# First adapter added to each tile of x instead of being folded into the weight product, and the sums of weight blocks made in one group instead of two

## The reference

```python
# layer 0: adapter alone, chosen for each batch by an id
x = x + ((x @ B0[id0].T) @ A0[id0].T)
# layer 1: weight, bias and adapter
x = x + (x @ W.T + b) + ((x @ lora_A[id1]) @ lora_B[id1]) * 2.0
```

## Time and profile before

| | |
|---|---|
| three runs | 1396.95, 1397.52, 1401.27 us |
| median | 1397.52 us |
| profiled execution | 1398.88 us, span 1396.9 us |
| mean granted TensorE clock | 0.997 |
| TensorE busy | 1372.8 us, 98% of the span |
| VectorE, ScalarE busy | 943.6 us (68%), 529.1 us (38%) |
| moved by DMA | 311.60 MB, mean 223 GB/s |

### The profile page before, as it was taken

One profiled execution on the slowest core, in us unless ns is written; L12 is line 12 of the kernel. 1 busy time (PEld: TensorE's weight loads), 2 busy tenths in 40 slices (PEclk: granted clock), 3 DMA queues, 4 the chain that ended last, 5 costly groups with the idle time before them and its releaser, 6 DMA issues.

```text
span 1396.9 us, 16200 instructions
## 1 busy us (share of the span) xinstructions
PE 1372.8 (98%) x6024; PEld 1128.8 (81%) x6024; DVE 943.6 (68%) x1049; ACT 529.1 (38%) x588; POOL 79.1 (6%) x163
## 2 busy tenths in 40 slices
PE   6899999999999999999999999999999999999999
PEld 5788877888888878888888888888888888888887
DVE  4677897777877887687765566665755566665662
ACT  3444444433334443343324453333233444333321
POOL 2012010001010000001001000000101000000000
PEclk9999999999999999999999999999999999999999
DMA  9789764778888987599895335455856343555642
GB/s 343 242 293 306 264 238 147 243 236 282 297 292 307 314 297 264 178 301 327 287 358 194 110 112 180 163 175 168 276 204 189 117 135 134 169 167 189 194 151 83
DMA packets 98591, 311.60 MB, mean 223 GB/s; under 512 B 13009, under 2 KB 14289, under 8 KB 98513
## 3 DMA queue, kind: packets, MB, share of 16 engines
q1 hardware_dynamic: 92736, 298.96, 63.1%
q0 software_dynamic: 5776, 11.61, 2.9%
HBM read 254.94 MB, written 55.57 MB: 222 GB/s over the span
## 4 chain that ended last, share of the span: by engine, by line
PE 91%; DVE 4%; DMA 2%; issue 1%; ACT 1%; SPq 1%; ACTq 0%; DVEq 0%
PE acc L590 27%; PE acc L591 27%; PE acc L592 27%; DMA w_two<-w 2%; PE acc L565 2%; PE down_ps L549 2%; PE down_ps L550 2%; PE image_ps L535 1%; PE image_ps L529 1%; PE image_ps L530 1%; DVE w_one L759 1%; DVE bg_lo L794 1%; DVE w_lo L767 1%; DVE x_lo L789 0%; ACT w_hi L627 0%
## 5 line engine op out<-in xcount | busy, mean ns | idle before, releaser
L590 PE MATMUL acc<-x_hi,w_hi 128*128 128x512 f32 x1792 | 702.1, 392 | 16.3 <-DVE x_lo L789 12.5
L591 PE MATMUL acc<-x_lo,w_hi 128*128 128x512 f32 x1792 | 699.5, 390 | 0.0
L592 PE MATMUL acc<-x_hi,w_lo 128*128 128x512 f32 x1792 | 699.1, 390 | 0.0
L627 ACT ACTIVATE w_hi<-w_one 128x1024 fp32r<-128x1024 f32 x223 | 235.9, 1058 | 541.1 <-PE acc L592 504.5
L767 DVE TENSOR_TENSOR w_lo<-w_one,w_hi 128x1024 fp32r<-128x1024 f32 x223 | 273.1, 1225 | 215.2 <-ACT w_hi L627 215.2
L590 PEld LDWEIGHTS acc<-x_hi,w_hi 128*128 128x128 f32 x1792 | 337.6, 188 | 89.0 <-issue 16.6
L591 PEld LDWEIGHTS acc<-x_lo,w_hi 128*128 128x128 f32 x1792 | 337.6, 188 | 71.7 <-issue 1.0
L592 PEld LDWEIGHTS acc<-x_hi,w_lo 128*128 128x128 f32 x1792 | 337.3, 188 | 71.2
L660 ACT ACTIVATE sums<-acc 128x512 f32<-128x512 f32 x96 | 57.1, 594 | 203.7 <-PE acc L592 188.1
L826 DVE SCALAR_TENSOR_TENSOR sums<-acc,bias_sb,sums 128x512 f32<-128x512 f32 x128 | 95.7, 747 | 22.0 <-PE acc L565 20.8
L759 DVE TENSOR_TENSOR w_one<-w_one,w_two 128x1024 f32<-128x1024 f32 x79 | 96.4, 1220 | 17.1 <-DMA w_two<-w 17.1
(11 more groups left out here) (61 smaller groups left out, 610.3 us busy)
## 6 DMA issues: line engine op xcount, KB each, us to landing
w_one<-w SPq DMA_DIRECT2D x143, 512.0 KB, 5.5
w_one<-w_sums SPq DMA_DIRECT2D x80, 512.0 KB, 3.7
w_two<-w SPq DMA_DIRECT2D x79, 512.0 KB, 7.4
x_stage<-x SPq DMA_DIRECT2D x64, 512.0 KB, 4.4
out<-sums SPq DMA_DIRECT2D x128, 256.0 KB, 4.6
w_sums<-w_one SPq DMA_DIRECT2D x40, 512.0 KB, 4.1
resident<-x SPq DMA_DIRECT2D x32, 512.0 KB, 8.6
bg_raw<-w_rows SPq DMA_DIRECT2D x32, 512.0 KB, 5.0
```

What stands on the lines that cost most here:

```text
L590: pe.matmul(ps[:, :], w_hi[ws][:, c, :], hi, start=(c == 0), stop=False)
L591: pe.matmul(ps[:, :], w_hi[ws][:, c, :], lo, start=False, stop=False)
L592: mm = pe.matmul(ps[:, :], w_lo[ws][:, c, :], hi, start=False, stop=(c == H - 1))
L627: act.activation(w_hi[s % W_PARTS][:, :, :], w_one[s % W_ONES][:, :, :], ACT.Copy).then_inc(w_hi_ready, 1)
```

## The change

Two things change, and the order tables with them.

1. The sums of W blocks are made in group 0 only and stored there (`KEPT_IN` is 0 for all); groups 1 to 3 load them.
2. The images of A0 through W are gone, with their 32 loads of `w_rows`, the splits and their matmuls. Instead, for each batch, an "up" projection (`project_up`: one matmul of 512 columns for each of the 16 tiles of 128 columns, L653) computes the first adapter's share, and VectorE (`add_up`) adds it from PSUM to the piece of x. Half of the pieces lie in `resident`; for each group 8 others (2 batches, 4 each) pass through `bg_raw`, are stored to a new DRAM tensor `x1` and loaded again where products 2, 3, 5 and 6 need them. Only the cross term of the two adapters is left of the images: 4 matmuls with `across` (`make_image`), steps 6 to 9.

So a batch's down projection, which needs all 16 tiles of x, must be complete before its x can be used: that of batch 1 stands ahead of step 0, and those of a later group move into products 4 to 6 of the group before.

```diff
-KEPT_IN = {0: 1, 1: 1, 2: 1, 4: 1, 6: 1}
+KEPT_IN = {0: 0, 1: 0, 2: 0, 4: 0, 6: 0}
...
+def downs(s):
+    if s >= STEPS:
+        return []
+    if s < 3:
+        first = (0, 8, 10, 13, 16)
+        return list(range(first[s + 1], first[s + 2]))
...
+def ups(s):
...
+    if s < 0:
+        return [0, 1]
+    g, i, o = where(s)
+    found = [2, 3] if s == 0 else []
+    if i == 0:
+        found += [16 * g + 4 * A0 + r for r, at in enumerate((1, 2, 4, 5) if g else (4, 4, 5, 5)) if at == o]
+    found += [16 * g + 4 * B0 + r for r, at in enumerate((7, 8, 10, 11)) if at == s % PER_GROUP]
...
+            def store_x1(v):
+                y = RAW["up", v]
+                n, half, r = up_chunk(v)
+                sp.wait_ge(up_added, 2 * v + 2)
+                sp.dma_start(x1[n][:, 2 * r:2 * r + 2, :], bg_raw[y % 2][:, :, :]).then_inc(x1_stored[y % 2], DMA)
...
+            def project_up(v):
...
+                for u in range(2):
+                    e = 2 * v + u
+                    if e >= 2:
+                        pe.wait_ge(up_added, e - 1)
+                    o = 2 * r + u
+                    pe.matmul(up_ps[e % 2][:, :], up_w[:, P * o:P * (o + 1)], rank_x_of(n)[:, :], start=True, stop=True)\
+                      .then_inc(up_done, 1)
...
+            def split_chunk(d):
+                wait_for_down_source(act, d)
+                for e in (2 * d, 2 * d + 1):
+                    if e >= 11:
+                        act.wait_ge(bg_used, e - 2)
+                    act.activation(down_parts(e)[0], down_source(e), ACT.Copy).then_inc(bg_hi_ready, 1)
...
+            for d in (5, 6, 7):
+                split_chunk(d)
+            make_w(1)
+            add_down(1)
+            split_rank_x(1)
+            for v in range(CH):
+                add_up(v)
+                split_x(0, v)
+            split_down(0)
+            for d in downs(0):
+                split_chunk(d)
```

More of the change, by code:

```diff
@@ L73, in turn @@
     return 2 * (n // 2) + 1 - n % 2
-def background(s):
+DOWN_STAGED = (2, 3, 14, 15)
+B1, A0, B0, A1 = range(4)
+def downs(s):
     if s >= STEPS:
         return []
+    if s < 3:
+        first = (0, 8, 10, 13, 16)
+        return list(range(first[s + 1], first[s + 2]))
     g, i, o = where(s)
[L81 to L90, removed]
@@ L93, in chunk @@
[L93 to L111, removed]
-def raw_loads(y):
-    return sum(raw_slot(u) == raw_slot(y) for u in range(y + 1))
@@ L119, in raw_before @@
[L119 to L126, removed]
-RANK_SPLIT = {(2, 7): 3, (4, 0): 4, (5, 0): 5, (6, 0): 6}
+    if g + 1 < GROUPS and H * 4 <= s % PER_GROUP < H * 5:
+        return [16 * (g + 1) + o]
+    if g + 1 < GROUPS and H * 5 < s % PER_GROUP <= H * 6:
+        return [16 * (g + 1) + 8 + s % PER_GROUP - H * 5 - 1]
@@ new lines, in down_chunk, with up_chunk, up_resident, down_resident @@
+def down_chunk(d):
+    return turn(d // 8), d % 8
+def up_chunk(v):
+    g, rest = divmod(v, 16)
+    part, r = divmod(rest, 4)
+    return 2 * g + (part in (B1, B0)), int(part in (B1, A1)), r
+def up_resident(v):
+    return v % 16 // 4 in (B1, A0)
+def down_resident(d):
+    n, k = down_chunk(d)
+    return n < 2 and (k >= 4) == (n == 1)
+RAW = {}
+for _s in range(-1, STEPS):
+    for _d in downs(_s):
+        if not down_resident(_d) and _d not in DOWN_STAGED:
+            RAW["down", _d] = len(RAW)
+    for _v in ups(_s):
+        if not up_resident(_v):
+            RAW["up", _v] = len(RAW)
@@ L130, in has_sum @@
+UP_SPLIT = {2: 1}
+UP_LOAD = {}
+for _g in range(GROUPS):
+    _s = PER_GROUP * _g
+    if _g:
+        UP_LOAD[_s - 15], UP_SPLIT[_s - 12] = 4 * _g + B1, 4 * _g + B1
+        UP_LOAD[_s - 7], UP_SPLIT[_s - 1] = 4 * _g + A0, 4 * _g + A0
+    UP_LOAD[_s + (3 if _g == 0 else 0)], UP_SPLIT[_s + 6] = 4 * _g + B0, 4 * _g + B0
+    UP_LOAD[_s + 7], UP_SPLIT[_s + 12] = 4 * _g + A1, 4 * _g + A1
+DOWN_AFTER = ((1, 3, 5), (5, 6))
+IMAGE_STEP = 6
 def has_sum(s):
@@ L443, in _ @@
                     store(s - 2)
[L444 to L449 removed]
+                for v in ups(s + 1):
+                    if not up_resident(v):
+                        load_raw("up", v)
+                if s + 2 >= CH:
+                    for d in downs(s + 2):
+                        load_raw("down", d)
             for s in (STEPS - 2, STEPS - 1):
@@ L499, in _ @@
                     .then_inc(a0_loaded, DMA)
-            for j in range(4):
-                load_rows(j)
-                if j:
-                    keep_image(j - 1)
+            load_up(1)
+            for n in range(NB):
+                pool.dma_start(rows[R * n:R * (n + 1), :], adapter(1, n, b1).rearrange("u r d -> (u r) d"))\
+                    .then_inc(b1_rows_loaded, DMA)
             for s in range(STEPS):
                 g, i, o = where(s)
-                if s + 4 in FIRST:
+                if s + 4 in FIRST and s:
@@ L775, in sum_x @@
                 if i == 1:
-                    for k in range(2):
-                        dve.wait_ge(resident_loaded[k][r], DMA * (g + 1))
+                    dve.wait_ge(up_added, up_number(p, r))
+                    if g == 0:
+                        dve.wait_ge(bg_ready, 32)
                     if last_staged(p, r) >= 0:
```

520 lines of the change are left out of this document (289 added, 231 removed).

## The result

The changed kernel took 1413.27 us (median of 4 runs, 1413.06 to 1415.06), the kernel before 1397.38 in the same comparison: ratio 1.011, interval [1.0091, 1.013]. It is slower by 1.1%, 14 us more than the 1399 forecast and 1 us above the upper end of the range.

A forecast was written before the change was run, and what follows sets the result against it. TensorE, busy 98% of the span, was taken as the bound. Step 1 at 55.5, matmuls of 1330.2 and 3.7 at the end made 1389.4; waits of 2, 3 and 4.2 gave 1398.6, median 1399 us, range 1387 to 1412.

The forecast's parts named there:

- The matmul count and its price: Whole kernel: 5816 matmuls from step 1 on at 0.2275 us each, 1323.1 us; 17.6 us less from matmuls removed and added.
- The start: Ahead of step 1: batch 1's down and up projections come first, so step 1 starts at 55.5, 34.7 us later.
- Waits in group 0: Group 0 after the start: three new waits of TensorE, 2, 3 and 4.2 us, 9.2 together.
- Steps 4 and 5: Group 0: the second up piece waits for VectorE's add of the first, behind `w_lo` and the sum; 3 us, ends 0 and 6.
- R1: Rival, slower: transfers set group 0's pace at 331 GB/s, wait 11 us, clock falls twice; 1412 us, chance 0.33.
- Transfers: Loops 9 to 20 of group 0: loads and stores run 11.2 us behind, 4.2 us of it waits; ends 0 and 11.
- the 7 us of cover: Group 0: transfer delay taken as hidden by weights issued early, VectorE's spare time and landing times; 7 us.
- Steps 1 and 2: Group 0: three down pieces a step with three half buffers make ScalarE's splits wait; 2 us for both, ends 0 and 5.
- R3: Rival, slower: VectorE bounds the first steps, in-order waits in product 0 cost 7 us more; 1406 us, chance 0.07.

The follow-up runs named there:

- e3: The kernel before with the sums of products 1, 2, 4 and 6 stored in group 0 and not made again in group 1: 1404.27 us.
- e4: The changed kernel with VectorE adding the two up shares ahead of the weights' sum in loops 4 and 5: 1409.85 us.
- e5: The changed kernel with the split of `up_w` put first in loop 6 and the four image-row copies at the start of their loops: 1414.74 us.
- e7: The changed kernel with a second new order ahead of step 0, all four up pairs before step 0 and the second weights' sum later: 1407.51 us.
- e10: The changed kernel with the orders of e7 and e4, two banks for image matmuls, the second sum and lora_A copy moved: 1402.57 us.
- e12: e11 with the copy of lora_A back at its old place on ScalarE, ahead of batch 0's rank rows: 1392.19 us.
- e6: The changed kernel with each sum's store cut to an eighth; groups 1 to 3 load one W block instead of the stored sum: 1407.25 us.
- e2: The changed kernel with sums of W blocks made in groups 0 and 1 and stored in group 1 only: 1415.05 us.
- e9: The changed kernel with the sums of products 1 and 2 made in every group and never stored: 1408.27 us.
- e1: The changed kernel with a first new order ahead of step 0, all down pieces split before the first weights are summed: 1410.19 us.
- e11: e10 and e9 together, so the sums of products 1 and 2 are not stored: 1395.33 us.

## Why the prediction was wrong

**What held.** The matmul count and its price: groups 1 to 3 took 989.9 us against 989. The start: 56.7 against 55.5, with the chain in the order given, 39.7 for the first step against 38. The adds are hidden in groups 1 to 3, and nothing came back in group 1 for the sums it no longer makes (e3 tested that part alone).

**The step that failed** is "Waits in group 0", three terms that came to 9.2 us. Group 0 lost 19.2 there:
- "Steps 4 and 5": the mechanism was right (e4 removed most of it), the size was not. 3 us were put, 6.9 measured. The add was late as worked out (1.9 us waited at 85.98), but batch 0's rank rows were late too, 1.4 us, and after these two waits the matmuls ran at the half clock, about 1.5 us (5.7 lost in step 4, against 4.2 in e5 and e7 with the same waits and no fall). The term left the clock out, although R1 priced it.
- Steps 7 and 8 had no term at all; they lost 4.6. Two new things meet there: the up matmul waits for `up_w`, whose last part stands behind the weights' sum on VectorE, and the second and third image matmuls wait for the copy of the one before out of the same bank. I had called the image matmuls unchanged. They stay four, but move from between the image pieces of four different steps to one bank in four steps in a row. Two banks took 3 us of the 4.6 away (e10, e12), the order of the copies 0.3 (e5).
- "Transfers": 4.2 put, 6.2 measured in steps 15 to 24, by the mechanism given. e6 shows that it is the bytes of the sums' stores, e2 that it moves with them, e9 that it goes with 16 of them. I had the rate as 350 GB/s; the stretches showed 370 and 344. So the rate was nearly right. That the 7 us of cover were too generous by 2 is the likely reading, and no run measured the cover.
- "Steps 1 and 2": 2 put, 0.6 measured.

The rest of the miss is 1.2 us of start, 1.3 spread over the rest of the span, and 1.6 between span and median: the median came 2.2 above the profiled span, where 0.6 had been put.

One of the prediction's own signs came: it called itself wrong if waits in steps 6 to 55 passed 8 us. The waits listed there are 8.4 us, the losses 11.7.

**The rivals.** The time came out where R1 had it, 1412, but for R1 in its own words (transfers set the pace) it is only a third right: 6.2 of the 19.2 us are transfers, and the clock fell in step 4, behind waits for VectorE. That the number agrees is luck. 11.5 us are lost in steps 4 to 8 by in-order waits for VectorE and by a bank, which is nearest to R3, priced 7 us and given a chance of 0.07; R3 named neither step 8 nor the bank. Taken together the forecast summed three waits at middling values, each with its upper end at 5, 6 and 11. The one of steps 4 and 5 came out above its upper end (6.9), the transfers in the middle (6.2), steps 1 and 2 near nothing, and one that was not on the list added 4.6. A dense stretch with four new kinds of work, all in order on three engines, should have weighed more than 0.40 together on the slow side.

**The Trainium skill** on transfers ("DMA: Bandwidth & Descriptors", "Bandwidth") gave 1394 by its 425 GB/s and 1397 by its 358. The changed kernel, with loads and stores, ran at 370 with the engines full and at 344 over the next 60 us, on both sides of the lower figure, so in such a mix the lower figure is the closer one; by neither figure would the steps 4 to 8 have been seen.

**What stays open.** Step 4 still loses 2.8 us and step 7 1.6 in the best version. Why two waits of the same lengths brought the half clock in the changed kernel and not in e5 and e7 isn't shown. The start is still 27 us behind the kernel before, and no run here tried to shorten its chain of single instructions (fewer copies for `rank_x`, a smaller first piece), so how much of that is bound to the scheme isn't known. Nor was the second order tried with fewer up pairs ahead of step 0.

## What to carry to other kernels

Replacing a large piece of work by a smaller one in a kernel that is bound by one engine brings only the difference on that engine (here 17.6 us), while each new dependence costs where the engine idles at the start or where an in-order queue puts a producer behind other work; list every new instruction that the bound engine waits for, with what stands ahead of it on its own engine, also those whose number does not change. Work saved on an engine that isn't the bound was worth nothing by itself here (e3), but it can be spent: making 48 sums again in place of storing and loading them took the bytes out of the stretch that was short of them. When a wait is removed by moving an instruction, look at what now stands behind it; four such moves here (in e1, e5, e7 and e10) gave some or all of their gain back close by.

## What the runs showed of the hardware

A mix of loads and stores of 512 KB ran at 370 GB/s with all DMA engines busy (120 to 160 in the changed kernel), and at 392 in a stretch in which they were mostly loads (the first row below). Whether TensorE waited did not follow from the rate alone: it waited for no transfer at 298 to 301 (e6), nor in the 40 us at 370, was idle 3.9 of the next 60 us at 344 (the changed kernel), and not at all in 25 us at 359 in the kernel before.

After waits of 1.4 and 1.9 us within 4 us, with six product matmuls between them, the granted clock was 0.83 over the ten microseconds from 80 to 90 in the changed kernel. In e7 TensorE had the same two waits with the same six matmuls between them, and the granted clock was 1.00 (second row). In e11 one wait of 2.36 us was followed by a granted clock of 0.51 over 7 us (third row), with matmuls 0.43 us apart. So waits shorter than the one of 2.84 us can bring the half clock, and the same waits don't always.

ScalarE's copy of 16 partitions by 1024 took 1.05 us, as long as one of 128 partitions (1.06), so the three pieces of `up_w` cost three full copies.

```profile
20.00:30.00 10.00, 6.14 (x13) 3.96 (x14) 8.78 (x12) 4.72 (x7) 2.16 (x4) 0.58 1.03 392
...
70.00:90.00 20.00, 16.60 (x87) 13.48 (x86) 13.86 (x17) 7.37 (x9) 1.46 (x3) 1.00 0.75 238
...
77.00:84.00 7.00, 6.66 (x17) 5.10 (x18) 3.60 (x6) 0.11 (x1) 0.00 (x0) 0.51 0.54 184
```
